# Reciprocals of the softmax row sums: written to memory in token order, read back contiguously

## The reference

```python
# x: (4, 1024, 256); 16 heads of 128 columns
q = rotary(proj(Wq, bq) * 128 ** -0.5)
k = rotary(proj(Wk, bk))
v = proj(Wv, bv)
sim = where(causal, -max, q @ k.T)
attn = softmax(sim, axis=-1)              # exp(sim - row max) / row sum
out = (attn @ v) @ Wo + bo
x = layernorm(x + out)
x = layernorm(x + ffn(x))                 # silu(gate) * up, then down, int8 weights
```

## Time and profile before

| | |
|---|---|
| time, three runs | 2212.37, 2212.69, 2213.2 us; median 2212.69 |
| span of the profiled execution | 2206.3 us |
| median minus that span | 6.4 us |
| PE busy | 2141.9 us (97%) |
| DVE busy | 1741.4 us (79%) |
| ACT busy | 1398.8 us (63%) |
| POOL busy | 1300.7 us (59%) |

### The profile page before, as it was taken

One profiled execution on the slowest core, in us unless ns is written; L12 is line 12 of the kernel. 1 busy time (PEld: TensorE's weight loads), 2 busy tenths in 40 slices (PEclk: granted clock), 3 DMA queues, 4 the chain that ended last, 5 costly groups with the idle time before them and its releaser, 6 DMA issues. The chain is left out here.

```text
span 2206.3 us, 48783 instructions
## 1 busy us (share of the span) xinstructions
PE 2141.9 (97%) x13640; PEld 1855.9 (84%) x13648; DVE 1741.4 (79%) x3035; ACT 1398.8 (63%) x3230; POOL 1300.7 (59%) x1080
## 2 busy tenths in 40 slices
PE   6999999999999999999999999999999999989997
PEld 5888888888888888888888888888888888867886
DVE  5788887788887888878888888788788888775776
ACT  4666666676666666666666666666666666654453
POOL 4566556676666665576665666565666666534554
PEclk8999999999999999999999999999999999999999
DMA  4422222233332222332233223223222232300000
GB/s 117 142 72 67 70 73 68 63 86 72 72 72 69 71 67 70 73 85 65 67 71 71 71 69 71 79 74 73 68 67 67 71 71 71 84 25 1 25 23 29
DMA packets 99870, 150.27 MB, mean 68 GB/s; under 512 B 31216, under 2 KB 35824, under 8 KB 99312
## 3 DMA queue, kind: packets, MB, share of 16 engines
q1 hardware_dynamic: 85856, 115.82, 21.6%
q10 hardware_dynamic: 13968, 33.95, 5.5%
HBM read 78.15 MB, written 4.46 MB: 37 GB/s over the span
## 5 line engine op out<-in xcount | busy, mean ns | idle before, releaser
L575 DVE TENSOR_TENSOR PT<-TP,PT 128x512 fp32r<-128x512 f32 (+3 forms) x768 | 421.6, 553 | 203.1 <-ACT PT L394 199.6
L519 ACT ACTIVATE prob<-S,neg_max 128x128 f32<-128x128 f32 (+7 forms) x512 | 380.7, 744 | 285.8 <-DVE neg_max L613 282.7
L394 ACT ACTIVATE PT<-TP 128x512 fp32r<-128x512 f32 (+3 forms) x768 | 362.6, 490 | 121.9 <-PE TP L818 116.2
L613 DVE TENSOR_REDUCE neg_max<-S 128x1 f32<-128x128 f32 (+7 forms) x512 | 380.7, 744 | 14.8 <-PE S L810 12.1
L339 POOL TENSOR_TENSOR swap<-swap,sin_t 128x512 f32<-128x512 f32 x256 | 348.0, 1359 | 70.3 <-DMA swap<-proj 69.8
L818 PE MATMUL TP<-ident,prob 128*128 128x128 f32 x2304 | 369.3, 274 | 0.5 <-ACT prob L519 0.5
L818 PEld LDWEIGHTS TP<-ident,prob 128*128 128x128 f32 x2304 | 273.6, 140 | 44.2 <-ACT prob L519 0.6
L350 POOL TENSOR_TENSOR QKB<-rot,QKB 128x512 fp32r<-128x512 f32 x128 | 172.9, 1350 | 218.2 <-ACT QKB L394 218.2
L640 DVE TENSOR_TENSOR rot<-rot,swap 128x512 f32<-128x512 f32 x256 | 278.5, 1088 | 7.6 <-POOL swap L339 7.2
L350 POOL TENSOR_TENSOR QKA<-rot,QKA 128x512 fp32r<-128x512 f32 x128 | 180.8, 1412 | 170.1 <-ACT QKA L394 170.1
L807 PE MATMUL S<-QKB 128*128 128x512 f32 (+3 forms) x1152 | 263.1, 355 | 1.3 <-ACT prob L519 1.3
(11 more groups left out here) (107 smaller groups left out, 4850.8 us busy)
## 6 DMA issues: line engine op xcount, KB each, us to landing
swap<-proj SPq DMA_DIRECT2D x512, 128.0 KB, 2.3
recip_b<-recip_d SPq DMA_DIRECT2D x128, 256.0 KB, 3.5
w_raw<-in_w_heads ACTq DMA_DIRECT2D x65, 384.0 KB, 3.0
wo_raw<-in_wo_heads ACTq DMA_DIRECT2D x32, 256.0 KB, 3.2
resid<-in_x_rows SPq DMA_DIRECT2D x4, 1024.0 KB, 10.9
out<-resid SPq DMA_DIRECT2D x8, 512.0 KB, 3.0
x_raw<-in_x_cols SPq DMA_DIRECT2D x3, 1024.0 KB, 5.1
recip_d<-recip SPq DMA_DIRECT2D x128, 2.0 KB, 1.8
```

Source lines behind the costliest of these rows:

```text
L394: copy = lambda o, i: nc.scalar.activation(o, i, ACT.Copy)
L519: nc.scalar.activation(prob[g][:, prob_at[g][i]:prob_at[g][i] + cols], S[s % 2][:, 0:cols], ACT.Exp, bias=neg_max[:, s:s + 1], scale=1.0, ...
L575: sub = lambda o, a, b: nc.vector.tensor_tensor(o, a, b, ALU.subtract)
L613: nc.vector.tensor_reduce(neg_max[:, s:s + 1], S[s % 2][:, 0:(s + 1) * P], AX.X, ALU.max, negate=True).then_inc(maxed, 1)
```

## The change

The write at line 298 puts the words into memory in token order, (t p): word t * 128 + p comes from partition p, column t. Neighbouring words in memory then come from different partitions, so each of the 512 words of 4 bytes is a piece of its own, where before there were 128 pieces of 16 bytes. The broadcast read at line 302 is the same. The normalisation now reads `recip_b`, O and writes `norm_o` all contiguously, 512 words a partition. No instruction is added, removed or moved on any engine.

```diff
                 if out_part:

                     sp.wait_ge(recip_ok, n_group(n, g))
-                    sp.dma_start(recip_d[g].rearrange("(p t) -> p t", p=P), recip[:, g, :]
-                                 ).then_inc(recip_out, 16)
+                    sp.dma_start(recip_d[g].rearrange("(t p) -> p t", p=P), recip[:, g, :],
+                                 allow_slow_non_contiguous=True).then_inc(recip_out, 16)
                 else:
                     sp.wait_ge(recip_out, 16 * n_group(n, g))
                     sp.dma_start(recip_b[:, g, :], recip_d[g:g + 1, :].to_broadcast([P, GQ])
@@
                         wait(dve, o_lo, n_group(n - 1, g) - 2)
-                        by_tile = lambda x: x.rearrange("d (t p) -> d t p", p=P)
-                        nc.vector.tensor_tensor(by_tile(norm_o[:, g, :]), by_tile(O[:, :]),
-                                                recip_b[:, g, :].rearrange("d (p t) -> d t p", p=P),
+                        nc.vector.tensor_tensor(norm_o[:, g, :], O[:, :], recip_b[:, g, :],
                                                 ALU.mult).then_inc(o_norm, 1)
```

## The result

| | before | after |
|---|---|---|
| time, median of four runs each (us) | 2212.53 | 2618.36 (2615.91 to 2620.0) |
| span of the profiled execution (us) | 2206.3 | 2614.1 |
| PE busy / idle in the span (us) | 2141.9 / 64.4 | 2275.1 / 339.0 |
| DVE busy (us) | 1741.4 | 1630.0 |

The ratio is 1.1841, with an interval of 1.1824 to 1.1858: 406 us more, where 2212.6 us had been forecast and 2252 us for the rival that pointed this way. The span grows by 407.8 us: PE waits 274.6 us more, and the same matmuls keep it busy 133.2 us longer.

What follows compares the result with a forecast made beforehand. PE's own work was taken to bound the repeated part; -0.4 and -0.1 us from normalisations at the end and +0.4 us from the write gave -0.1 us on 2212.69: 2212.6 us, range 2210.8 to 2216.5.

Steps and rivals of the forecast that it cites:

- What bounds the kernel: Repeated part, 200 to 1800 us: PE's own work sets the end, busy 1590.89 of 1600 us.
- the sum: Whole span: -0.4 and -0.1 us from shorter normalisations at the end, +0.4 us from the write at the start: -0.1 us.
- The normalisation's length: The 128 instructions of L621: from 1096 to 687 ns each, 52 us less DVE busy time.
- The write's landing: Write of the reciprocals to memory: 0.4 us longer, bounds 0.2 and 5.4 us, on a landing of 1.8 us.
- The threshold: Group 0, write to read: landing can grow from 2.3 to about 6.1 us before an even stage gets longer.
- The late rival: Write lands past 6.1 us, the excess paid in 31 even stages: 34 us, plus 5.4 at the start, 2252 us; chance 0.05.
- More to spare: Group 1: write and read stand in two different steps, so it has more reserve than group 0's 2.8 us.
- DVE and POOL in another order: Even stages: POOL starts first, L640 about 100 ns longer on the mean; if not hidden, 9 us, 2222 us; chance 0.06.
- The regular wait gone: Step 4 of odd stages, before L833: PE loses its 8 us of idle time, 2204.5 us; chance 0.07.
- The growth at the start: Stage 0: the longer write delays the loads and swap PE waits for, once, by 0.4 us, bounds 0.2 and 5.4.
- Both signs: Forecast wrong if DVE waits for recip_b in every stage, or PE's repeated-part idle time moves by more than 4 us.
- the reserve: Group 0's way from write to normalisation: 2.8 us to spare, plus PE's 0.64 us and DVE's 0.41 us.

Runs made afterwards that it cites:

- e1_norm_flat: Kernel before with only the normalisation reading contiguously and the old write kept (output wrong): 2208.69 us against 2212.09, ratio 0.9987.
- e7_words_apart: Changed kernel with the 512 written words 64 bytes apart in memory, the read fetching words that are not the reciprocals: 2208.47 us, ratio 1.0004.
- three writes: Kernel before with its old write of 16-byte pieces issued three times, each behind the landing of the one before: 2353.13 us, ratio 1.0649.

## Why the prediction was wrong

**What bounds the kernel** was right: PE's own work, with one small regular wait. It was also the reason to believe that a shorter DVE instruction is worth next to nothing, and the normalisation alone confirmed that (0.9 to 5.1 us by the interval of `e1_norm_flat`, none that can be seen in `e7_words_apart`, against -0.5 us in the sum).

**The normalisation's length** was right: 687 ns forecast, 691 measured. The row beside it with the same form was the right witness, although it adds where the normalisation multiplies; of the two pages of the Trainium skill quoted, the one on 16-byte lines agrees in direction. The other says that odd strides work in the mode of one result a cycle; that they cost nothing there was the prediction's reading of it, and 1096 against 691 ns doesn't bear it out.

**The write's landing** is the step that failed. The way to memory of 1.8 us was to grow by 0.2 us at least (packets) and by 5.4 at most (the whole landing four times as long), and 0.4 was taken. It grew by about 7 us, to some 9 with the 0.33 us of issue in it. Both ends of that bound scaled with the number of pieces. The probes show that the number is not the variable: 512 apart take 1.9 us, 64 side by side 6.2. The text had said that nothing excludes a slower word, and "no row here shows a transfer of that kind"; then the upper end was not a bound, and should not have been treated as one. The Trainium skill's factor of 19 named the right side, and would have given 34 us, four times too much; it compares with the hardware's transpose, not with a write in another order, so the prediction stretched it. What it says of one descriptor for each element agrees with the 512 packets, but 512 packets alone were not slow.

**The threshold** was about right for group 0. It lay at 6.1 us between write and read, and 9.1 us passes it by 3.0. PE's waits for PT at this place grew from 20.0 to 206.8 us, which is 3.0 us in each of 62 stages. That the two agree so well is partly luck: the read, 1.7 us later as well, is not in it, and the stages themselves are longer, which gives time back. With three writes, at 5.6 us and a read 0.8 us later, these waits had grown by 25 us only.

**The price per microsecond** failed as well. The late rival charged 31 even stages with what lies beyond the threshold. Its own 34 us was too low as it stood: it set 7.2 us, from the page's 1.8, against a threshold counted from 2.3; the same growth of 5.4 us gives 7.7, and 31 x 1.6 = 50 us. By the formula 9.1 us would have given 31 x 3.0 = 93 us. Measured were 406. What was left out:

- The odd stages pay too. DVE waits for group 0 in 62 stages, not 31; the longer slack of two output products was not enough (in the stage after the one shown, PE waits 2.73 us at 1256.00).
- Group 1 pays. "More to spare" was true by 3 us (11.7 against 8.55 us from write to need), which is not enough for 9 us of landing and 5 of read. The swaps behind its write and behind its read are late too: POOL waits 335.2 us for them, where it was 69.8. Alone this costs 32 us, beside group 0 more.
- The read itself lands in 5.2 us and not 3.5.
- PE's clock. Each wait of PE can be followed by a stretch in which the granted clock is at the lower level, 0.50 of full speed, that is 1.2 GHz instead of 2.4. The sum had no term for that. The mean granted clock is 0.937 where it was 0.991; as an estimate, 2141.9 us of busy time at the one become 2265 at the other, 123 of the 133.2 us by which the matmuls are busy longer. That is about a third of the loss.

The last point as stretches of the changed kernel (columns as in the earlier trace rows). PE waited 3.03 us up to 1202.31; the clock fell in that wait and was at 0.50 in every stretch behind it up to 1208.00, the last of which is shown. Behind the wait of 2.27 us at 1220.00 it stayed at 1.00:

```profile
1198.00:1200.00 2.00, 1.28 (x10) 0.83 (x8) 0.00 (x0) 1.22 (x3) 1.03 (x2) 1.00 0.57 209
1200.00:1202.30 2.30, 0.00 (x0) 0.00 (x0) 1.48 (x4) 0.71 (x2) 0.35 (x1) 0.89 0.35 124
...
1205.00:1208.00 3.00, 3.00 (x10) 2.25 (x9) 1.75 (x4) 1.76 (x6) 1.27 (x1) 0.50 0.03 0
...
1220.00:1221.00 1.00, 1.00 (x5) 0.82 (x6) 1.00 (x2) 0.20 (x1) 0.72 (x1) 1.00 0.00 0
```

**The other rivals.** DVE and POOL in another order: L640 was to take 100 ns more. With the contiguous normalisation alone it takes 1105 ns instead of 1088, 17 more, so the order hardly changed; in the changed kernel it takes 816, I take it because DVE and POOL meet less often once both wait. The regular wait gone: no. **The growth at the start** (0.4 us once, behind the loads of `resid`): PE's wait there is now 6.63 us instead of 3.70, a growth of 2.9 us and not 0.4, within the bounds of 0.2 and 5.4.

**The chances.** Both signs that the forecast is wrong came: DVE waits for `recip_b` in 62 stages, and PE's idle time between 200 and 1800 us grew by 183.5 us. The late landing had 0.05. The mechanism was written down with its place and its threshold, and the reserve, "more than twice today's landing", was the argument against it. That argument needs a witness for the landing, and there was none.

## What to carry to other kernels

When a change turns a DMA into a kind that no row of the trace shows, its landing has no upper bound from the rows; then the reserve decides, and with a reserve of a few microseconds and a round trip in every stage a loss should not be put at 0.05. Ask of a write not only how many pieces it has but whether many neighbouring words in memory are each a piece of its own: here a write in pieces of 16 bytes, paid for by a strided read on an engine that has time, was the better order. And price a wait of the busiest engine above its length: here each microsecond of PE's idle time came with half a microsecond of slower matmuls (274.6 and 133.2 us), and with 0.4 to 0.6 in the five other kernels here that lost more than 1%.

## What the runs showed of the hardware that was not expected

- 512 words of 4 bytes written to neighbouring places in memory land in 7.8 to 10.4 us over three probes, though their packets are through in 1.5 (in the changed kernel, from 1203.8 us on); 64 bytes apart they land in 1.8 to 2.0 (2.3 to 2.6 with a partition's four words next to each other in that row), and as 128 pieces of 16 bytes mostly in 1.4.
- 16 neighbouring words are harmless (1.3 us), 32 take 2.9 to 5.1 us, 64 take 6.0 to 7.5, 128 take 7.4 to 8.2.
- Four columns of 128 neighbouring words took 3.9 us into one partition of on-chip memory and 8.1 to 9.6 us to memory.
- A transfer issued behind such a write can land late too: a swap was in use 7.8 us after its issue, where another in the kernel before took 2.9 (those of 1227.11 and 1006.59 us).
- A row of 2 KB broadcast from one partition of on-chip memory to 128 takes 11.2 us, from memory 3.0 to 4.1.
- A step of four words in one operand of a DVE instruction on 128x512 in float32 costs 0.4 us (1096 and 691 ns).
